# Two-layer graph network on one core: the four engines' hand-written orders rearranged, and the setup cut into pieces

## The reference, cut to what matters

```
h   = gat(gat(x))          # two graph attentions: softmax over masked scores, times W h
x1  = norm0(x + h);  x2 = norm1(x1 + relu(x1 @ w_ff1 + b) @ w_ff2 + b)      # layer 0
att = sum over r of (softmax(q k^T) * (adj == r)) @ v_r, 8 heads            # layer 1
x3  = norm2(x2 + att @ Wo + b);  out = norm3(x3 + gelu(x3 @ W1 + b) @ W2 + b)
```

## Time and profile before

| | |
|---|---|
| time, median of 3 runs | 3114.9 us (3109.67 to 3115.02) |
| the profiled execution | 3114.71 us |
| its span, first to last instruction | 3112.9 us |
| PE busy | 3017.0 us (97%), 26980 matmuls |
| ACT, DVE, POOL busy | 2429.1, 2237.8, 1889.4 us |
| mean granted TensorE clock | 0.987 |

### The profile page before, as it was taken

The page is one execution under the profiler, slowest core; times in us unless marked ns, Lnnn a source line. Parts: engine busy times, 40 slices in busy tenths (PEclk is TensorE's granted clock), DMA queues, the critical chain, the costliest instruction groups (busy, mean ns, idle before and its releaser), DMA issues.

```text
span 3112.9 us, 78634 instructions
## 1 busy us (share of the span) xinstructions
PE 3017.0 (97%) x26980; PEld 2712.3 (87%) x26980; DVE 2237.8 (72%) x4975; ACT 2429.1 (78%) x6218; POOL 1889.4 (61%) x1747
## 2 busy tenths in 40 slices
PE   5899999999999999999999999999999999999996
PEld 5788888888888888888889889889889889889885
DVE  4677777777777777777777777777777777777763
ACT  3578878878878878878878878888888887787874
POOL 3365665665665665665665665665666666666663
PEclk7999999999999999999999999999999999999998
DMA  4000100100100100100100100100100100100100
GB/s 144 25 22 24 34 27 24 34 27 24 34 27 24 34 27 24 34 27 24 34 27 24 34 27 24 34 27 24 34 27 24 34 27 24 34 27 24 34 12 14
DMA packets 101943, 93.54 MB, mean 30 GB/s; under 512 B 14736, under 2 KB 101008, under 8 KB 101776
## 3 DMA queue, kind: packets, MB, share of 16 engines
q1 hardware_dynamic: 101904, 93.00, 9.8%
HBM read 76.17 MB, written 16.78 MB: 30 GB/s over the span
## 4 chain that ended last, share of the span: by engine, by line
PE 87%; DVE 5%; issue 3%; ACT 3%; POOL 1%; DVEq 0%; DMA 0%; POOLq 0%; SPq 0%; ACTq 0%
PE ps_f L290 11%; PE ps_f L292 10%; PE ps_f L291 10%; PE ps_ao L496 8%; PE ps L290 5%; PE ps L291 5%; PE ps L292 5%; PE ps L476 4%; PE ps L486 4%; PE ps_ao L543 4%; PE ps_g L292 3%; PE ps_g L291 3%; PE ps_g L290 3%; PE ps_ao L290 2%; ACT norm L696 2%
## 5 line engine op out<-in xcount | busy, mean ns | idle before, releaser
L1038 POOL TENSOR_TENSOR hid_lo<-hid_full,hid_hi 128x512 fp32r<-128x512 f32 x512 | 694.0, 1359 | 372.0 <-ACT hid_hi L659 354.6
L1015 POOL TENSOR_TENSOR rstd<-vareps,neg_half 128x2 f32<-128x2 f32 x256 | 218.2, 852 | 613.5 <-DVE vareps L832 613.5
L290 PE MATMUL ps_f<-down_w_hi,hid_hi 128*128 128x256 f32 x2048 | 588.3, 287 | 1.3 <-POOL hid_lo L1038 1.3
L291 PE MATMUL ps_f<-down_w_lo,hid_hi 128*128 128x256 f32 x2048 | 570.4, 279 | 0.0
L292 PE MATMUL ps_f<-down_w_hi,hid_lo 128*128 128x256 f32 x2048 | 570.1, 278 | 0.0
L676 ACT ACTIVATE prob<-ps,s_least 128x256 f32<-128x256 f32 x1024 | 469.5, 489 | 5.9 <-DVE s_least L880 5.1
L290 PEld LDWEIGHTS ps_f<-down_w_hi,hid_hi 128*128 128x128 f32 x2048 | 385.5, 188 | 23.4 <-issue 19.9
L880 DVE TENSOR_REDUCE s_least<-ps 128x4 f32<-128x1024 f32 x256 | 309.9, 1211 | 124.3 <-PE ps L476 124.2
L292 PEld LDWEIGHTS ps_f<-down_w_hi,hid_lo 128*128 128x128 f32 x2048 | 388.1, 189 | 0.0
L291 PEld LDWEIGHTS ps_f<-down_w_lo,hid_hi 128*128 128x128 f32 x2048 | 385.9, 188 | 0.0
L659 ACT ACTIVATE hid_hi<-hid_full 128x512 fp32r<-128x512 f32 x512 | 323.9, 633 | 16.2
(11 more groups left out here) (161 smaller groups left out, 9580.2 us busy)
## 6 DMA issues: line engine op xcount, KB each, us to landing
adj_in<-adj_keys SPq DMA_DIRECT2D x128, 256.0 KB, 2.8
xT_in<-x_features SPq DMA_DIRECT2D x64, 256.0 KB, 2.7
norm<-x_nodes SPq DMA_DIRECT2D x64, 256.0 KB, 2.7
out_nodes<-norm SPq DMA_DIRECT2D x64, 256.0 KB, 2.1
row_vectors<-all_row_vectors SPq DMA_DIRECT2D x1, 1536.0 KB, 11.1
raw_up<-L_w_ff SPq DMA_DIRECT2D x1, 1024.0 KB, 8.4
raw_down<-L_w_ff SPq DMA_DIRECT2D x1, 1024.0 KB, 9.6
raw_v<-L_Wv SPq DMA_DIRECT2D x4, 256.0 KB, 10.2
```

The source lines that it names most:

```text
L290: nc.tensor.matmul(ps_out, left[0], right[0], start=first, stop=False)
L291: nc.tensor.matmul(ps_out, left[0], right[1], start=False, stop=False)
L1038: pool.tensor_tensor(hid[1][:, 2 * m:2 * m + 2, :], hid_full[:, 2 * m:2 * m + 2, :], value(hid[0][:, 2 * m:2 * m + 2, :]), ALU.subtract).t ...
```

## The change

It has two parts. The banks that each helper uses are the same before and after; no arithmetic is added or taken away.

**The bodies.** On PE, `pe_up(., 0, 1)` and `pe_up(., 0, 2)` move to the end of the body before; `pe_scores(b, 1)` comes first; `pe_turn(d, 2)` moves from the first to the third place among the four quarters of `pe_down(a, 0)`; `pe_up(d, 1, 1)` moves ahead of `pe_av_all(b, 0)`; `pe_gat_mix(c, 1)` moves ahead of `pe_up(d, 1, 3)`, and `pe_gat_rows(e)` ahead of a quarter of `pe_down`. On ACT, `act_prob(b, 1, 0)` moves ahead of norm2's end, and the copies `act_gat_wh` move behind a norm's end. On DVE, `dve_gat_wh(c, 0)` moves to the end of the body before, `dve_adj_top` to the start of the next one, the mask of the second head group ahead of `dve_norm(c, 0)`, the fence and the split of x behind it, and `dve_gat_wh(c, 1)` ahead of `dve_turned(a, 1)`. On POOL, both last affines (norm 2 and 3) leave the place ahead of `pool_hidden(d, 1, 0)` for places behind `pool_gat_in` and `pool_rstd(d, 3)`; the rest keeps its sequence, with the body's boundary moved.

**The setup.** `raw_a` gets an event of its own, so that PE starts when the two weights are there; DVE copies the transposed weight first; the second half of the folding (`dve_both_setup`) moves behind the fence and the split of graph 0. The q, k and v setup is cut in pieces: on PE from one block in body -2 to three blocks in bodies -2 and -1, on DVE and ACT likewise.

```diff
 def pe_body(...)
-            if ff0:
-                pe_up(pe, a, 0, 1)
-                pe_up(pe, a, 0, 2)
-                pe_up(pe, a, 0, 3)
             if att1:
                 pe_scores(pe, b, 1)
             if ff0:
+                pe_up(pe, a, 0, 3)
                 pe_down(pe, a, 0, 0, 0)
...
                 pe_gat_mix(pe, c, 0)
...
-            if ff1:
-                pe_turn(pe, d, 2)
             if ff0:
                 pe_down(pe, a, 0, 0, 1)
                 pe_down(pe, a, 0, 1, 0)
+            if ff1:
+                pe_turn(pe, d, 2)
+            if ff0:
                 pe_down(pe, a, 0, 1, 1)
             if gat:
                 pe_gat_wh1(pe, c, 1)
-                if isinstance(t, int) and t == -2:
-                    pe_qkv_setup(pe)
+                if isinstance(t, int) and t == -1:
+                    pe_qk_setup(pe)
...
                 pe_turn(pe, a, 1)
+                if isinstance(t, int) and t == -1:
+                    pe_v_setup(pe, 1)
             if ff1:
                 pe_up(pe, d, 1, 0)
+                pe_up(pe, d, 1, 1)
             if att1:
                 pe_av_all(pe, b, 0)
...
             if ff1:
-                pe_up(pe, d, 1, 1)
                 pe_up(pe, d, 1, 2)
+            if gat:
+                pe_gat_mix(pe, c, 1)
+                if isinstance(t, int) and t == -2:
+                    pe_v_setup(pe, 0)
+            if ff1:
                 pe_up(pe, d, 1, 3)
-            if gat:
-                pe_gat_mix(pe, c, 1)
...
+            if nxt:
+                pe_gat_rows(pe, e)
             if ff1:
                 pe_down(pe, d, 1, 1, 0)
             if nxt:
-                pe_gat_rows(pe, e)
                 pe_gat_cols(pe, e)
...
                 pe_prob_turn(pe, a, 0, 1)
+            if gat:
+                pe_up(pe, c, 0, 1)
+                pe_up(pe, c, 0, 2)
 def act_body(...)
+            if att1:
+                act_prob(act, b, 1, 0)
             if ff1:
                 act_norm_end(act, d, 2)
                 act_turned(act, d, 2)
             if att1:
-                act_prob(act, b, 1, 0)
                 act_prob(act, b, 1, 1)
...
             if nxt:
-                act_gat_wh(act, e, 0)
                 act_gat_pre(act, e, 0)
...
                 act_norm_end(act, d, 3)
+            if nxt:
+                act_gat_wh(act, e, 0)
 def dve_body(...)
-            if gat:
-                dve_gat_wh(dve, c, 0)
+            if att1:
+                dve_rec(dve, b, 0, 0)
+            if gat:
                 dve_gat_split(dve, c, 0)
+                if isinstance(t, int) and t == -1:
+                    dve_qkv_lo_setup(dve)
+            if att1:
+                dve_least(dve, b, 1, 0)
+                dve_adj_top(dve, b)
+                dve_rec(dve, b, 0, 1)
+            if gat:
+                dve_gat_wh12(dve, c, 1)
                 if isinstance(t, int) and t == -2:
                     dve_qkv_setup(dve)
-                    dve_rows_setup(dve)
...
+            if gat:
+                dve_gat_wh(dve, c, 1)
             if ff0:
                 dve_turned(dve, a, 1)
...
             if att1:
                 dve_ao(dve, b, 0)
+                dve_mask(dve, b, 1)
+            if gat:
+                dve_norm(dve, c, 0)
             if nxt:
                 dve_fence(dve, e)
-            if gat:
-                dve_norm(dve, c, 0)
-            if nxt:
                 dve_gat_in(dve, e)
...
                 dve_turned(dve, c, 0)
                 if isinstance(t, int) and t == -2:
-                    dve_qkv_bias_setup(dve)
-                    dve_qkv_lo_setup(dve)
+                    dve_rows_setup(dve)
...
+                dve_gat_wh(dve, e, 0)
             if att1:
                 dve_norm(dve, b, 2)
 def pool_body(...)
+            if ff0:
+                pool_hidden(pool, a, 0, 3)
+            if att1:
+                pool_rec_wide(pool, b, 0)
+                pool_affine(pool, b, 1)
+            if ff0:
+                pool_rstd(pool, a, 1)
+            if att1:
+                pool_rec_wide(pool, b, 1)
...
+            if ff1:
+                pool_affine(pool, d, 2)
             if gat:
                 pool_affine(pool, c, 0)
...
                 pool_rstd(pool, d, 3)
+                pool_affine(pool, d, 3)
...
-                pool_hidden(pool, c, 0, 3)
-            if ff0:
-                pool_rec_wide(pool, a, 0)
-                pool_affine(pool, a, 1)
-            if gat:
-                pool_rstd(pool, c, 1)
-            if ff0:
-                pool_rec_wide(pool, a, 1)
-            if att1:
-                pool_affine(pool, b, 2)
-            if ff1:
-                pool_affine(pool, d, 3)
 def pe_gat_setup(pe):
-            pe.wait_ge(gat_in.sem, 48)
+            pe.wait_ge(gat_in.sem, 32)
 def dve_gat_setup(dve):
-            dve.wait_ge(gat_in.sem, 48)
+            dve.wait_ge(gat_turned.sem, 1)
+            dve.tensor_copy(raw_turned[:].rearrange("p k n -> p (k n)"), ps_f[:, 0, :]).then_inc(gat_step.sem, 1)
+            dve.wait_ge(gat_in.sem, 32)
+            dve.wait_ge(a_in.sem, 16)
...
+        def dve_both_setup(dve):
             dve.wait_ge(gat_step.sem, W_BOTH)
-            scores(raw_both, 1, D)
+            dve_scores_setup(dve, raw_both, 1, D)
```

More of the change, by code:

```diff
@@ L561, in pe_body @@
                     pe_up_setup(pe, 1)
+            if ff0:
+                pe_down(pe, a, 0, 0, 1)
+                pe_down(pe, a, 0, 1, 0)
             if ff1:
@@ L951, in dve_body @@
             if att1:
+                dve_rec(dve, b, 1, 0)
                 dve_rec(dve, b, 1, 1)
@@ L959, in dve_body @@
                 dve_v_more(dve, b)
+            if gat:
+                dve_gat_wh(dve, c, 1)
             if ff0:
                 dve_turned(dve, a, 1)
+                if isinstance(t, int) and t == -1:
+                    dve_qk_bias_setup(dve)
             if att1:
@@ L976, in dve_body @@
             if nxt:
+                dve_fence(dve, e)
                 dve_gat_in(dve, e)
                 if isinstance(t, int) and t == -3:
+                    dve_both_setup(dve)
                     dve_up_setup(dve, 0)
-            if att1:
-                dve_mask(dve, b, 1)
             if ff0:
@@ L1100, in sp_setup @@
                 sp.dma_start(raw_gat[l][:], rows(p0[f"W{l + 1}"])).then_inc(gat_in.sem, 16)
-            sp.dma_start(raw_a[:], across(vectors[15 * D:19 * D])).then_inc(gat_in.sem, 16)
+            sp.dma_start(raw_a[:], across(vectors[15 * D:19 * D])).then_inc(a_in.sem, 16)
             sp_features(sp, 0)
@@ L1140, in pe_gat_setup, with dve_scores_setup @@
             pe.wait_ge(gat_step.sem, GAT_READY)
+        def dve_scores_setup(dve, weights, l, at):
+            for half in range(2):
+                for k in range(C):
+                    dst = raw_both[:, k, at + 1 - half:at + 2 - half]
+                    dve.tensor_tensor_reduce(out=raw_prod[:, l, half, k, :], in0=weights[:, k, 0:D],
+                                             in1=raw_a[:, (2 * l + half) * D:(2 * l + half + 1) * D], scale=1.0,
+                                             scalar=0.0, op0=ALU.mult, op1=ALU.add,
+                                             accum_out=dst).then_inc(gat_step.sem, 1)
         def dve_gat_setup(dve):
-            dve.wait_ge(gat_in.sem, 48)
+            dve.wait_ge(gat_turned.sem, 1)
+            dve.tensor_copy(raw_turned[:].rearrange("p k n -> p (k n)"), ps_f[:, 0, :]).then_inc(gat_step.sem, 1)
+            dve.wait_ge(gat_in.sem, 32)
+            dve.wait_ge(a_in.sem, 16)
             dve.tensor_scalar(raw_a[:], raw_a[:], -1.0, None, ALU.mult).then_inc(gat_step.sem, 1)
             dve.wait_ge(gat_step.sem, TURNED_A)
-            def scores(weights, l, at):
-                for half in range(2):
-                    for k in range(C):
-                        dst = raw_both[:, k, at + 1 - half:at + 2 - half]
-                        dve.tensor_tensor_reduce(out=raw_prod[:, l, half, k, :], in0=weights[:, k, 0:D],
-                                                 in1=raw_a[:, (2 * l + half) * D:(2 * l + half + 1) * D], scale=1.0,
-                                                 scalar=0.0, op0=ALU.mult, op1=ALU.add,
-                                                 accum_out=dst).then_inc(gat_step.sem, 1)
-            scores(raw_gat[0], 0, D + 2)
-            dve.wait_ge(gat_turned.sem, 1)
-            dve.tensor_copy(raw_turned[:].rearrange("p k n -> p (k n)"), ps_f[:, 0, :]).then_inc(gat_step.sem, 1)
+            dve_scores_setup(dve, raw_gat[0], 0, D + 2)
             dve.wait_ge(gat_turned.sem, 2)
             dve.tensor_copy(raw_both[:, :, 0:D], ps_ao[:, 0, :].rearrange("p (k n) -> p k n", n=D)).then_inc(gat_step.sem, 1)
+        def dve_both_setup(dve):
             dve.wait_ge(gat_step.sem, W_BOTH)
-            scores(raw_both, 1, D)
+            dve_scores_setup(dve, raw_both, 1, D)
             dve.wait_ge(gat_step.sem, WA)
```

(20 more changed lines are left out.)

36 lines of the change are left out of this document (12 added, 24 removed).

## The result

The changed kernel is slower: 3146.36 us median (3139.66 to 3147.59), ratio to the kernel before 1.0103, 95% interval 1.0087 to 1.0118. I had forecast 3074, with 0.90 on faster.

What follows compares the result with a forecast made beforehand. PE's instruction list was taken to bound the loop. From 3114.71 us, 28 for the bodies (62 x 0.45) and 14 for the setup came off, plus 1 for the drain: 3073.7, stated as 3074; range 3050 to 3102 (0.85).

Steps and rivals of the forecast that it cites:

- the term for DVE: DVE's masks, fence and dve_adj_top in the body: they move in DVE's free time, at a cost of 0.
- "+0.05 (0 to +0.5)" for `pe_v(b, 0)`: PE, behind the later pe_turn(d, 2): hT_lo[2] ends about when PE needs it, +0.05 us a body.
- a new wait of over 0.65 us a body: Anywhere in the loop: only a new wait of this size would make the forecast wrong in sign.
- My rival for slower: pe_qk waits for ACT's last activation of pe_up(d, 1, 3); a body loses 1.1 us, 3139 us, chance 0.06.
- L510: In pe_av_all(b, 0), formerly L509: early pe_up(d, 1, 1) covers the wait on hT_lo, -0.40 us a body.
- the downs around `turn(d, 2)`: PE's pe_down(a, 0): 24 products ahead of the turn now follow products directly, -0.10 us taken of -0.17.
- norm1's wait: PE ahead of pe_turn(a, 1): its chain is not shortened, so the 0.33 us stay (between -0.33 and +0.15).
- the first rival: pe_gat_rows(e) waits 0.2 to 0.5 us for gT_lo and returns loop gain: 3086 to 3101 us, chance 0.20.
- The setup: Before the loop: earlier transposes, q, k, v in pieces and later biases save 13 to 14 us by its end.
- The drain: Last bodies: ACT's four exponentials and DVE's adj_top come earlier, mostly falling on waits, +1 us (0 to +2).

Runs made afterwards that it cites:

- small_affine1: Changed kernel with POOL's affine(b, 1) cut to 32 of 256 columns per row block, so its result differs: 3097.7 us.
- new_setup_old_body: New setup code with the four engines' body orders of the kernel before: 3101.3 us.
- small_affine1_t1: small_affine1 with one idle extra transpose at L510: 3084.8 us.
- turn_old: Changed kernel with PE's turn(d, 2) and ACT's norm2 end and copy back at their old places: 3146.0 us.
- new_setup_up_early: new_setup_old_body with only PE's up(d, 1, 1) moved ahead of av_all(b, 0): 3099.7 us.
- up_early_t1: new_setup_up_early with the first transpose of L510 done once more, as idle work: 3084.2 us.
- up_early_t2: new_setup_up_early with the first transpose of L510 done twice more, as idle work: 3091.0 us.
- mask_first_t1: mask_first with one idle extra transpose at L510: 3116.1 us.
- mask_first: Changed kernel with DVE's mask(b, 0) ahead of the wh12(c, 1) copy instead of behind it: 3116.0 us.

## Why the prediction was wrong, point by point

**The step that failed** is the term for DVE, in which the masks, the fence and `dve_adj_top` "move in DVE's free time", put at 0, and with it "+0.05 (0 to +0.5)" for `pe_v(b, 0)`. The free time is there (DVE is idle for 1.69 us ahead of `wh12`), but the mask stands behind `wh12`, not in it, beside POOL's affine, and ahead of `hT_lo[2]`, which I had seen to have a margin of about nothing. The term measured +0.97. The prediction said that only a new wait of over 0.65 us a body could turn the sign; this was one, at a place where it didn't look. I had read the rows of that same effect and applied it to one spot only, the fence and cast, and not to every DVE operation whose neighbour on POOL changed. My rival for slower (3139, chance 0.06) named another wait, ahead of `pe_qk`; it didn't come, and that its time lies near the measured one is chance.

**The second miss** is that I took a product at 113 ns wherever it follows a product. Body by terms, before to after: L510 -0.43 (forecast -0.40), the downs around `turn(d, 2)` -0.10 (-0.10), `pe_v` +0.97 (+0.05), `turn(a, 1)` -0.18 (0: since PE comes later, norm1's wait shrinks), and +0.26 for the rest, which is mostly pace. Over the 226 products a body that follow a product, the mean spacing rose from 114.8 to 115.4 ns, +0.14 in all; the -0.10 of the downs is contained in that, so the others lost 0.24. The long run at 117.8 in 20 of 55 bodies is 0.14 of it. Sum +0.52. The -0.10 came out as forecast, but by the pace: 24 downs at 113.3 in place of 117.8.

**Right:** the wait of L509 goes; norm1's wait stays, 0.33, where nothing else is late (small_affine1); `pe_gat_rows(e)` has its `gT_lo` in time, so the first rival stays out. **The setup**: `pe_gat_rows` starts at 15.52 (forecast 16), the `wh12` copy of graph 1 at 52.32 (52). Of the 12.5 us won there 11.4 are left at the first `pe_wo` in new_setup_old_body and 9.9 in after. How much too large the term of 13 to 14 was, if at all, these single executions don't tell: with the same setup code that matmul comes anywhere from 135.98 (small_affine1_t1) to 143.73 us (turn_old), the mean granted clock of the first 100 us was 0.86 in after, 0.72 in turn_old, 0.91 in new_setup_old_body and 0.71 before, and the medians put new_setup_old_body 13.6 us below before. **The drain** cost 3.9, not 1. In turn_old it is 2.7, but three kernels that differ only by idle transposes (new_setup_up_early, up_early_t1, up_early_t2) lie 1.5 us apart in it, 121.7 to 123.1, so the 1.2 can't be put down to the turn. small_affine1 has 125.1, as long as after without the collision of the masks with the full affine; which of the moves costs the rest I didn't separate.

**Open:** what sets the pace. I compared the long run's with that in which the products of `up(d, 1, 1)` ended, some 2.2 us earlier. Where L510's two transposes follow these directly (nine kernels, after among them), the long run took the other pace of the two in 478 of 493 bodies. With one or two idle transposes at L510 it took the same pace in 222 of 223 bodies of four kernels, but in only 30 of 56 of mask_first_t1. What in the engine does so, no run here shows, nor why mask_first_t1 differs.

## What to carry to other kernels

When an order is changed, list for each DVE operation with two inputs in SBUF which POOL operations it will now lie beside, and price both at the sum of the two; then see what stands behind each in its queue. Here these are the mask and `adj_rest`. `att_s_hi` belongs on the list too, though it reads one tensor (1.95 us against 0.61); `least` and `hT_lo`, which read PSUM, weren't slowed. The faster kernel here keeps the old orders, takes the new setup, the one early `up(d, 1, 1)`, and an idle transpose: 3084.2 us, 0.9910 of before. When a removed wait doesn't pay, look at the spacing of the instructions that follow it, not only at the waits.

## What was not expected of the hardware

- A POOL operation on 64 columns took 1.30 us beside a DVE mask of 1.3 to 1.4; POOL copies 256 columns in 0.40.
- Runs of matmuls with 256 columns have two paces, 113.3 and 117.8 ns, at a granted clock of 1.00. One more transpose of 0.11 us ahead of such a run made a body of new_setup_up_early 0.26 us shorter, and left that of mask_first as it was.
- Before, all bodies are 46.813 or 46.820 us; with a pace drawn anew in each they spread over 0.23 us in after (47.22 to 47.45).
